# A gate stage with three blocks under way, scan operands fetched in mid-unit, and triangular systems inverted by blocks

## Time and profile before

| | us |
|---|---|
| median of 3 runs | 5948.83 (5944.33 to 5955.05) |
| profiled execution, its time | 5938.72 |
| its span, first to last instruction | 5936.9 |
| scan, first instruction of SP to the last state | 990.5 to 2465 |
| gate, first DMA to the last store | 2484 to 2763 |

### The profile page before, as it was taken

One profiled execution on the slowest core, in us unless ns is written; L12 is line 12 of the kernel. 1 busy time (PEld: TensorE's weight loads), 2 busy tenths in 40 slices (PEclk: granted clock), 3 DMA queues, 4 the chain that ended last, 5 costly groups with the idle time before them and its releaser, 6 DMA issues. The chain is left out here.

```text
span 5936.9 us, 198550 instructions
## 1 busy us (share of the span) xinstructions
PE 5334.8 (90%) x71072; PEld 4594.3 (77%) x71072; DVE 3954.2 (67%) x12333; ACT 3351.7 (56%) x9514; POOL 2458.2 (41%) x3584
## 2 busy tenths in 40 slices
PE   6888886888888888664999999999969999999999
PEld 5888885888888888543788788787757777777777
DVE  4666665898888898443666666666636666666665
ACT  4777774444444444343666666666636666555665
POOL 1222223677777777200343333343323444434443
PEclk8999998999999999866999999999989999999999
DMA  2334334556656655454000000000010000000000
GB/s 72 92 93 99 89 94 104 127 127 133 135 124 131 135 127 128 97 186 137 13 13 15 13 13 16 13 13 15 11 44 19 22 19 19 19 19 19 22 19 16
DMA packets 999453, 386.78 MB, mean 65 GB/s; under 512 B 775664, under 2 KB 948592, under 8 KB 998512
## 3 DMA queue, kind: packets, MB, share of 16 engines
q1 hardware_dynamic: 998192, 384.92, 26.6%
q10 hardware_dynamic: 1088, 0.00, 0.0%
HBM read 216.46 MB, written 168.30 MB: 65 GB/s over the span
## 5 line engine op out<-in xcount | busy, mean ns | idle before, releaser
L1717 POOL TENSOR_TENSOR l_pn<-l_prob,l_rinv 128x512 f32<-128x512 f32 x512 | 532.2, 1039 | 1266.8 <-DVE l_rinv L1817 1262.8
L2035 ACT ACTIVATE l_prob<-l_prob,l_nb,l_rq 128x256 f32<-128x256 f32 x1024 | 604.4, 592 | 281.0 <-DVE l_nb L1837 280.5
L1304 DVE TENSOR_TENSOR sc_sol<-sc_sol,sc_step 128x15 f32<-128x15 f32 (+7 forms) x960 | 326.6, 340 | 33.0
L1300 DVE TENSOR_TENSOR sc_step<-sc_prob,sc_sol 128x15 f32<-128x15 f32 (+7 forms) x960 | 329.8, 344 | 26.6
L1066 POOL TENSOR_TENSOR sc_ax<-sc_late,sc_headmask 128x256 f32<-128x256 f32 x256 | 171.3, 669 | 401.7 <-DMA sc_tok<-scratch_tok 361.5
L1195 ACT ACTIVATE sc_d_qk<-sc_part,sc_headmask 128x64 f32<-128x64 f32 x1024 | 270.2, 336 | 42.0 <-DMA sc_part<-scratch_part 42.0
L1125 PE MATMUL sc_AB<-sc_early,sc_bx 64*64 64x64 f32 x4096 | 176.8, 224 | 123.2 <-POOL sc_kx L1066 107.0
L1730 POOL TENSOR_TENSOR l_outt<-l_t,l_xat 128x256 f32<-128x256 f32 x64 | 46.4, 725 | 553.8 <-DVE l_t L1899 553.8
L1195 ACT ACTIVATE sc_d_qb<-sc_part,sc_headmask 128x64 f32<-128x64 f32 x1024 | 271.6, 339 | 0.0
L1242 ACT COPY sc_y<-sc_Y 128x64 f32<-128x64 f32 x256 | 54.3, 212 | 361.8 <-PE sc_Y L1133 361.8
L1125 PEld LDWEIGHTS sc_AB<-sc_early,sc_bx 64*64 64x64 f32 x4096 | 153.6, 140 | 129.5 <-issue 129.1
(11 more groups left out here) (353 smaller groups left out, 17918.7 us busy)
## 6 DMA issues: line engine op xcount, KB each, us to landing
scratch_cm<-cm SPq DMA_DIRECT2D x64, 512.0 KB, 4.1
sc_early<-scratch_cm SPq DMA_DIRECT2D x128, 256.0 KB, 3.2
scratch_part<-sc_att SPq DMA_DIRECT2D x64, 512.0 KB, 4.3
sc_part<-scratch_part SPq DMA_DIRECT2D x64, 512.0 KB, 5.2
scratch_tok<-vt SPq DMA_DIRECT2D x512, 48.0 KB, 1.8
l_h<-scratch_h SPq DMA_DIRECT2D x128, 129.0 KB, 2.6
scratch_gr<-gr SPq DMA_DIRECT2D x64, 256.0 KB, 2.0
sc_late<-scratch_cm SPq DMA_DIRECT2D x64, 256.0 KB, 4.0
```

The lines of the kernel that those rows point to most:

```text
L1300: nc.vector.tensor_tensor(prod, prob[k][:, m:m + 1, m + 1:CH].broadcast_to([P, rows, cols]), x[:, 0:rows, m:m + 1].broadcast_to([P, rows, ...
L1304: ins = nc.vector.tensor_tensor(x[:, 0:rows, m + 1:CH], x[:, 0:rows, m + 1:CH], prod, ALU.add)
L1717: tt(pn[s][:, pair], prob[s][:, pair], rinv[s][:, pair].unsqueeze(2).broadcast_to([P, 2, 2 * P]), ALU.mult).then_inc(Q["pn"][s].sem, 1)
L2035: last_ = nc.scalar.activation(prob[s][:, h], prob[s][:, h], ACT.Exp, scale=rq8[s][:, h:h + 1], bias=nb[s][:, h:h + 1], accum_out=sums[s][ ...
```

## The change

Three edits, in two stages.

1. The late operands are loaded two units ahead and not one, in the middle of SP's unit, behind the first `early` and `v` loads of that unit; the first two units' loads are issued at the start of the stage.
2. `solve` has four parts, one for each chunk. Part 0 adds the identity to the systems and solves the four 4 x 4 blocks on the diagonal at once (2 steps of a product and a sum, on 8 elements or fewer for each partition, views `n4`, `x4`). Parts 1 to 3 fill the off-diagonal blocks as `X11 N12 X22`: each product of two blocks is one multiplication over a cube (row, column, inner index; the right-hand block is read down its columns, so that neighbouring reads are 16 elements apart) and one sum over the innermost index. Part 1 makes both 4 x 4 blocks (cubes of 64), part 2 the first product of the 8 x 8 block (a cube of 512) and part 3 the second.
3. `gate_stage` works on units of one window with both batches in one instruction where the form allows it (`z1`, `z` and `xa` on 128 x 512). In each slot of the loop an engine does a phase of the new unit, one of the unit before it and one of the unit before that. There are two buffers, and PSUM has a tile of its own for `y`, the projection and `x`.

```
@@ scan_stage, SP: order of a unit
                     if exists(w, k, 1):
                         n1 = shift(w, k, 1)
-                        load_late(*n1)
                         load_part(*n1)
                         load_t(*n1)
                         load_gl(*n1)
...
                         if exists(w, k, 1):
                             load_v(*shift(w, k, 1), j)
+                        if j == 0 and exists(w, k, 2):
+                            load_late(*shift(w, k, 2))
@@ scan_stage, DVE
-                for m in range(m0, m1):   (one product and one sum each, m = 0..14)
+                def cube(dst, lhs, rhs, n):
+                    both = [P, n, n, n]
+                    return nc.vector.tensor_tensor(dst.rearrange("p (r t m) -> p r t m", r=n, t=n), lhs.unsqueeze(2).broadcast_to(both),
+                                                   rhs.rearrange("p m t -> p t m").unsqueeze(1).broadcast_to(both), ALU.mult)
...
+                    if part_ == 0:
+                        nc.vector.tensor_tensor(x16, n16, eye[:], ALU.add).then_inc(s_chain, 1)
+                        for m in (1, 2):
+                            nc.vector.tensor_tensor(prod, n4[:, :, m:m + 1, m + 1:4].broadcast_to(both), x4[:, :, 0:m, m:m + 1].broadcast_to(both), ALU.mult)
+                            nc.vector.tensor_tensor(x4[:, :, 0:m, m + 1:4], x4[:, :, 0:m, m + 1:4], prod, ALU.add).then_inc(s_chain, 1)
+                    if part_ == 1:   (2 cubes of 64, 1 sum to 32, 2 cubes of 64, 2 sums to 16)
...
+                    if part_ == 2:
+                        cube(step_[:], x16[:, 0:8, 0:8], n16[:, 0:8, 8:16], 8).then_inc(s_chain, 1)
+                        nc.vector.tensor_reduce(half_[:], step_[:].rearrange("p (n m) -> p n m", m=8), AX.X, ALU.add).then_inc(s_chain, 1)
+                    if part_ == 3:
+                        cube(step_[:], half_[:].rearrange("p (r m) -> p r m", m=8), x16[:, 8:16, 8:16], 8).then_inc(s_chain, 1)
+                        nc.vector.tensor_reduce(x16[:, 0:8, 8:16], step_[:].rearrange("p (r t m) -> p r t m", r=8, t=8), AX.X, ALU.add)
@@ gate_stage: the slots (new unit u, u-1, u-2)
+  PE:  turn_y(u); project(u-1); turn_x(u-2)
+  ACT: normed(u); modulated(u-2); inv_std(u-1)
+  DVE: normalized(u-2); gated(u); residual(u-1)
+  SP:  load_y(u+2); load_gr(u+2); store_xa(u-1); load_x(u+1); store_h(u-2)
```

More of the change, by code:

```diff
@@ new lines, in slot @@
+                def slot(k, i, new=True, old=True, older=True, more=True):
+                    if new and more:
+                        load_y(k, i + 1)
+                        load_gr(k, i + 1)
+                    if old:
+                        kk, ii = before(k, i, 1)
+                        store_xa(kk, ii)
+                        if more:
+                            load_x(kk, ii + 1)
+                    if older:
+                        store_h(*before(k, i, 2))
+                sp.dma_start(wo[:], a["wo_attn"]).then_inc(s_c, 16)
@@ new lines, in _ @@
+                for k in range(2):
+                    load_y(k, 0)
+                    load_gr(k, 0)
+                    load_x(k, 0)
+                slot(0, 0, older=False, old=False)
+                slot(1, 0, older=False)
+                with sp.Fori(1, LAST) as i:
+                    slot(0, i)
+                    slot(1, i)
+                slot(0, LAST, more=False, older=False)
+                load_x(1, LAST)
+                store_h(0, LAST - 1)
+                slot(1, LAST, more=False)
@@ L1452, in _, with slot @@
+                def slot(k, i, new=True, old=True, older=True):
+                    if new:
+                        normed(k, i)
+                    if older:
+                        modulated(*before(k, i, 2))
+                    if old:
+                        inv_std(*before(k, i, 1))
                 act.preload_act_table_set(LN_EXP)
@@ new lines, in normalized, with slot @@
+                def normalized(k, i):
+                    dve.wait_ge(S["rstd"][k].sem, S["rstd"][k].after(i))
+                    dve.wait_ge(S["xT"][k].sem, S["xT"][k].after(i, 1))
+                    for b in range(NB):
+                        last_ = nc.vector.tensor_scalar(xn[k][:, b], xa[k][:, b], mv[k][:, b, 0:1], rstd[k][:, b:b + 1], ALU.subtract, ALU.mult)
+                    last_.then_inc(S["xn"][k].sem, 1)
+                def slot(k, i, new=True, old=True, older=True):
+                    if older:
+                        normalized(*before(k, i, 2))
+                    if new:
+                        gated(k, i)
+                    if old:
+                        residual(*before(k, i, 1))
@@ new lines, in turn_x, with slot @@
+                def turn_x(k, i):
+                    pe.wait_ge(S["xn"][k].sem, S["xn"][k].after(i))
+                    pe.wait_ge(S["h0"][k].sem, S["h0"][k].after(i, 1))
+                    for b in range(NB):
+                        for c in range(CC):
+                            at = b * C + c * P
+                            last_ = nc.tensor.transpose(x_ps[k][:, at:at + P], xn[k][:, b, c * P:(c + 1) * P], ident[:])
+                    last_.then_inc(S["xT"][k].sem, 1)
+                def slot(k, i, new=True, old=True, older=True):
+                    if new:
+                        turn_y(k, i)
+                    if old:
+                        project(*before(k, i, 1))
+                    if older:
+                        turn_x(*before(k, i, 2))
```

304 lines of the change are left out of this document (162 added, 142 removed).

## The result

| | before | after |
|---|---|---|
| median of 4 runs on the same chip, us | 5947.74 (5944.33 to 5955.05) | 5691.26 (5688.41 to 5696.22) |
| ratio, with 95% interval | | 0.9568 (0.9552 to 0.9585) |
| profiled execution, us (span) | 5938.7 (5936.9) | 5688.4 (5686.6) |

The forecast was 5706 us, with a range of 5630 to 5800. The change takes off 256 us, 243 were forecast.

What follows compares the result with a forecast made beforehand. No scan engine was full, DVE and PE near it; a chain of phases bound the gate. Scan units 147, scan start 12, last units 6 and gate 78 sum to 243 us: 5948.8 to 5706, eight-in-ten range 5630 to 5800.

Steps and rivals of the forecast that it cites:

- Part 1, the late load: Scan: loading two units ahead removes POOL's wait, 5.7 us a unit, at no cost for SP; DVE is late next.
- Part 2, the solve: Scan: DVE's solve falls from 11.8 to 5.4-8.4 us a unit; the unit from 22.15 to 19.7, 147 us in all.
- rival A: Scan: cubes are slow from reads at a stride of 16 elements; unit 21 to 21.7 us, time 5790 to 5830; chance 0.14.
- rival C: Scan: reaches PE's floor as DVE's contended prices fall into PE's slack; 210 us instead of 147, time 5643; chance 0.10.
- 147 + 6: Scan after the first state sum: 147 us from shorter units over 60 units, 6 us from the last units.
- Contention: Scan: busy POOL slows DVE instructions with two SBUF inputs, `d_t` 0.42 to 0.83 us, taking back part of the solve's gain.
- POOL's total of 16.1 us leaves 3.6 a unit in which it regains its lead: Scan: argument that POOL's work leaves slack in a 19.7 us unit, against SP's mid-unit wait making PE stall.
- Part 3, the gate: Gate stage: bound by its chain of phases; 32 one-window slots of 5.8 us make 201 us against 279, 78 us less.
- DMA's "5.2 to 6.7": Gate slot: 1.58 MB takes 5.2 us at the best stretch's 306 GB/s, 6.7 at an ordinary busy stretch's 234.
- rival B: Gate stage: DMA holds it with only two buffers; slot 7.0 us, gate 39 us less, time 5745; chance 0.10.
- D: Scan: SP waits mid-unit for POOL's buffer, delayed loads stall PE; at 5 us a stall, time 6005; chance 0.03.
- E: Scan: late load still late, behind four `y` stores; POOL's wait halves, unit about 20.8 us, time 5772; chance 0.05.

Runs made afterwards that it cites:

- e1: Kernel before with only the late operands loaded two units ahead, in mid-unit; 5889.14 us, ratio 0.9909.
- e4: Changed kernel with the cubes' right-hand block read along its rows, so multiplying by the transposed block; 5690.61 us, ratio 0.9574.
- e6: Changed kernel with the expansion of `d_t` moved from DVE to ACT, in four instructions of 64; 5687.59 us, ratio 0.9567.
- e8: Changed kernel with the off-diagonal parts 1 to 3 of `solve` left out, systems not fully inverted; 5680.9 us, ratio 0.9554.
- e9: Changed kernel with the even units' four `y` stores moved from the unit's end to mid-unit; 5685.36 us, ratio 0.9575.
- e7: Changed kernel with each gate slot loading `gr` a second time into a tile nobody reads; 5750.46 us, ratio 0.9671.
- e5: Changed kernel with the late load, still two units ahead, issued at the head of SP's unit; 5758.5 us, ratio 0.9679.
- e2: Kernel before with only the new `solve` by blocks, late load still one unit ahead at the head; 5989.23 us, ratio 1.0078.
- e3: Kernel before with only the new `gate_stage`, scan as before; 5845.11 us, ratio 0.9838.
- e10: Changed kernel with even units' `y` stores in mid-unit and the deviation from the mean made in one instruction; 5673.12 us, ratio 0.9553.
- e11: Kernel before with only the new `solve`, plus the even units' `y` stores moved to mid-unit; 5968.39 us, ratio 1.0052.

## Why the prediction was right

**Part 1, the late load: right, and half of a pair.** POOL's wait went, at no cost for SP in mid-unit. That the kernel then hangs on DVE is e1 (21.4 a unit). The prediction gave one sum for both edits and did not ask what each would do alone; part 2 alone is +44 us.

**Part 2, the solve: size right, its shape partly, and with luck.** 8.1 us a unit were measured where the working had 5.4 free and 8.4 with POOL always busy, and I had said that POOL would be busy for most of it. The cube is at 1.23 us near the 1.4 of the working for another reason: not 0.7 doubled by POOL, but 0.35 for the stride, which the working left to rival A, and 0.2 for POOL. The unit is 19.72 (forecast 19.7). The four intervals were given for full contention as 5.3, 4.95, 4.6 to 5.1 and 4.7 to 5.2; measured are 5.46, 4.56, 4.67 and 5.02. The second was too long: DVE's prices there fell into PE's slack. So the unit is a mixture of the forecast (0-1 and 3-0) and of rival C (1-2 and 2-3). Two figures of that working do not add up: the terms given for 0-1 make 5.5 and not 5.3, and the masked product stands in them at 0.34 where the earlier trace rows have 0.415. The two diagonals had 1.55 at the slow price, and take 1.32. That the whole met 19.7 to 0.02 us is in part luck: the working derives it from DVE's load, but three runs that take work from DVE (e4, e6, e8) stay at 19.6 to 19.8. With DVE relieved the wait for the early load, costed at nothing, comes to 1.0 us a unit (e8, 19.60); with that wait gone and DVE's work as it was the unit is 19.61 (e9). So two bounds stand at nearly the same height, and the working had one of them. No run relieves both, and whether the unit would then reach PE's 18.65 is open. From the first to the last state sum 147 + 6 = 153 us were forecast and 150.4 measured; the scan's start gave 9.1 for 12.

**Contention: there, smaller on DVE than priced, and it goes both ways.** `d_t` has a mean of 0.687 us (0.657 before), with POOL busy nearly always; most of them take 0.62 and not 0.83 us. What I did not see: POOL pays too. Its groups in the kernel before and then in the changed one, both from 1600 to 2200:

```profile
L1087 POOL TENSOR_TENSOR sc_bT<-sc_tok,sc_headmask 128x128 f32<-128x128 f32 x216 | 92.7, 448 | 0.0
L1087 POOL TENSOR_TENSOR sc_kT<-sc_tok,sc_headmask 128x128 f32<-128x128 f32 x216 | 84.5, 410 | 0.0
```

```profile
L1089 POOL TENSOR_TENSOR sc_kT<-sc_tok,sc_headmask 128x128 f32<-128x128 f32 x243 | 146.6, 622 | 0.0
L1089 POOL TENSOR_TENSOR sc_bT<-sc_tok,sc_headmask 128x128 f32<-128x128 f32 x244 | 131.1, 556 | 0.0
```

The step "POOL's total of 16.1 us leaves 3.6 a unit in which it regains its lead" is wrong: POOL is busy 570.2 of 600 us, 18.7 a unit, and leaves one. The unit came out as forecast all the same: with POOL at 546 or 525 us (e4, e8) it is hardly shorter. With the cubes read in rows (e4) it is 546 us, and with the cubes left out (e8) 525, `kT` at 0.44 us again; `ax` and `kx`, of 256 elements, cost no more than before.

**Part 3, the gate: the mechanism right, the slot too long.** Forecast were 201 us for the 279 of before, with a slot of 5.8; measured are 98 us less, which is 181. The timeline of DVE's residual, once a slot:

```profile
2336.01 0.69 DVE L1578 TENSOR_TENSOR ga_xa<-ga_O,ga_xt 128x512 f32<-128x512 f32 x1 [0.94 <-PE ga_O L1628]
...
2494.64 0.68 DVE L1578 TENSOR_TENSOR ga_xa<-ga_O,ga_xt 128x512 f32<-128x512 f32 x1
```

That is 31 slots of 5.12 us. 32 x (5.8 - 5.12) = 22 us are the missing ones. The term that failed is DMA's "5.2 to 6.7": the 6.7 came from an ordinary stretch at 234 GB/s, in which DMA was busy for 0.69 only. The stage is at 0.90 and 269 GB/s over its length, and the row of the whole stage had it already: 181 GB/s at a share of 0.56 is 323 GB/s at a full share, 4.9 us a slot. The allowance for engines that rub (0.6) was not needed. The wait that held the stage before, `ga_lnv` for `ga_mv`, is 11.2 us in all. What PE waits for now, 2330 to 2500, is the load:

```profile
PE ga_Y L1620 <- DMA ga_yt<-scratch_y_tok: 50.5, 28, 3.4
```

So rival B's cause is the right one (DMA holds the gate, e7), at a better price than B had.

**Rivals in the scan.** A: by the Trainium skill's rule on 16-byte lines (SBUF — State Buffer, "Door 1: The DMA port swizzle") the strided reads would pay. The runs agree on the direction, 1.23 us for 0.88, and the kernel does not feel it. D: real at the unit's head (e5), absent in mid-unit. E: absent, no wait of `sc_ax` for `sc_tok` is left.

**Not foreseen: the local layers.** They are 11.2 us longer, with no edit in them. Over 1520 us from the stage's head PE waits 4.7 us in 16 times in the changed kernel for something that took 0.9 us in 2 times before:

```profile
PE l0B L2297 <- DVE l_pT L1961: 4.7, 16, 0.7
```

The first layer took 1566 to 1568 us in before, e1, e2, e3, e6, e8, e10 and e11, and 1573 to 1577 in the changed kernel, e4, e5, e7 and e9; the second 1591 to 1593 in before, e1, e2, e3, e6, e10 and e11 and 1595 to 1602 in the others. It goes with the build and not with the stage that was edited. The cause was not tried and stays open; it is as large as the differences between e4, e6, e8, e9 and e10, so those are read by the scan's intervals and not by the totals. These too move by 0.13 to 0.15 us a unit without an edit (e7, e3), so the units of e4, e6, e8, e9 and e10 can't be told from the changed kernel's. The layers also hide a miss in the total: the gate gave 20 us more than forecast and they took 11 back.

## What to carry to other kernels

When two waits take turns in one loop, price them together: alone the first edit here gave 56 us, the second cost 44, and both gave some 156. A total that meets the forecast does not show that its working did: take the term away that the sum rests on, as e8 does, and see whether the time moves. Shortening the engine that only delays the one behind it can turn its slack into one long stall of TensorE a unit, which here cost clock as well as time. For a stage that is to be bound by DMA, divide the rate by the busy share over the whole stage of before; where a load waits for a buffer, put it where the buffer is free, not as early as possible.

## What the runs showed of the hardware

- In e2, from 1600 to 2200 us, each stall of TensorE of 3.3 us or more had the granted clock at 0.5 (1.2 GHz) beside or behind it, at the place shown for the next four groups of matmuls (0.86 us apart for 0.47); in all the low level had 64.8 us of 600. Stalls of up to 1.7 us had none.
- VectorE and GpSimd slow each other: `kT` on GpSimd went from 0.41 to 0.62 us when VectorE's cubes came beside it (0.44 with the cubes left out), a VectorE product with two SBUF inputs from 0.42 to 0.83, in most cases of the changed kernel to 0.62. Sums of 512 elements stayed at 0.69 us, and the masked product from PSUM at 0.42.
- A VectorE product of 512 float32 whose one input is read 64 bytes apart took 1.23 us, and 0.88 read along the rows, both beside a busy GpSimd; with GpSimd idle the first took 1.03.
